# The mask of every other pair of heads added to the bias by GpSimd instead of by a TensorE product

## What is computed

```python
q = (x @ Wq + bq).reshape(B, S, N_HEAD, HEAD_DIM).transpose(0, 2, 1, 3)
k = (x @ Wk + bk).reshape(B, S, N_HEAD, HEAD_DIM).transpose(0, 2, 1, 3)
v = (x @ Wv + bv).reshape(B, S, N_HEAD, HEAD_DIM).transpose(0, 2, 1, 3)
scores = jnp.einsum('bhqd,bhkd->bhqk', q / math.sqrt(HEAD_DIM), k)
scores = scores + attention_bias
scores = jnp.where(src_mask, -jnp.inf, scores.astype(jnp.float32))
probs = jax.nn.softmax(scores, axis=-1).astype(v.dtype)
ctx = jnp.einsum('bhqk,bhkd->bhqd', probs, v)
x = x + (ctx.transpose(0, 2, 1, 3).reshape(B, S, D) @ Wo + bo)
h = _ln(x) * g2 + beta2
return x + (_gelu2(h @ W1 + b1) @ W2 + b2)
```

## Time and profile before

| | us |
|---|---|
| median of 3 runs | 1448.05 |
| lowest and highest | 1447.22 and 1448.72 |
| the profiled execution | 1434.4 |
| its span, which the rows refer to | 1432.6 |

### The profile page before, as it was taken

One profiled execution on the slowest core, in us unless ns is written; L12 is line 12 of the kernel. 1 busy time (PEld: TensorE's weight loads), 2 busy tenths in 40 slices (PEclk: granted clock), 3 DMA queues, 4 the chain that ended last, 5 costly groups with the idle time before them and its releaser, 6 DMA issues. The chain is left out here.

```text
span 1432.6 us, 34478 instructions
## 1 busy us (share of the span) xinstructions
PE 1273.8 (89%) x9923; PEld 1165.2 (81%) x9923; DVE 990.3 (69%) x2766; ACT 899.0 (63%) x2318; POOL 664.5 (46%) x580
## 2 busy tenths in 40 slices
PE   5874899999999999935799999899998999999996
PEld 4774899999999999934587888778887877788875
DVE  5776788879887888646565667666765667666652
ACT  3442777778777877711666676666665666667661
POOL 2775577777777777742132332322332232331211
PEclk9999999999999999967999999999999999999998
DMA  5885121221112112146766555655665556654620
GB/s 194 270 269 188 43 65 48 57 63 55 55 49 64 55 47 65 42 153 196 226 200 200 178 180 192 215 185 171 185 205 185 171 180 204 203 189 149 192 68 15
DMA packets 184851, 203.18 MB, mean 142 GB/s; under 512 B 18192, under 2 KB 172752, under 8 KB 184720
## 3 DMA queue, kind: packets, MB, share of 16 engines
q1 hardware_dynamic: 170832, 163.14, 36.8%
q10 hardware_dynamic: 7712, 21.89, 4.8%
q0 software_dynamic: 6176, 16.79, 3.3%
HBM read 155.89 MB, written 41.68 MB: 138 GB/s over the span
## 5 line engine op out<-in xcount | busy, mean ns | idle before, releaser
L1224 ACT ACTIVATE bias<-bias,neg_max 128x256 f32<-128x256 f32 x512 | 255.4, 501 | 207.6 <-DVE neg_max L1536 207.0
L343 POOL TENSOR_TENSOR w_lo<-w,w_hi 128x512 fp32r<-128x512 f32 x156 | 241.2, 1567 | 0.0
L1536 DVE CUSTOM_DVE_ANT_0 bias<-ps_s,bias 128x256 f32<-128x256 f32 x512 | 194.3, 417 | 28.6 <-PE ps_s L1312 11.1
L745 DVE TENSOR_TENSOR w_lo<-w,w_hi 128x512 fp32r<-128x512 f32 x156 | 149.9, 1000 | 70.2 <-ACT w_hi L423 68.6
L544 PE MATMUL ps_y<-w_hi,hidT_hi 128*128 128x256 f32 x624 | 180.1, 289 | 1.9 <-DVE token_rows L759 1.9
L531 PE MATMUL ps_h<-htokT_hi,w_hi 128*128 128x256 f32 x624 | 178.4, 286 | 3.2 <-DVE htokT_lo L750 3.2
L1310 PE MATMUL ps_s<-mask_f,minus_ident 128*128 128x256 f32 x512 | 154.9, 324 | 28.5 <-DVE neg_max L1536 16.3
L1176 POOL TENSOR_TENSOR act_lo<-up_f,act_hi 128x512 fp32r<-128x512 f32 x64 | 82.6, 1290 | 208.4 <-ACT act_hi L1268 208.4
L531 PE MATMUL ps_h<-htokT_lo,w_hi 128*128 128x256 f32 x624 | 178.2, 286 | 0.0
L531 PE MATMUL ps_h<-htokT_hi,w_lo 128*128 128x256 f32 x624 | 178.0, 285 | 0.0
L544 PE MATMUL ps_y<-w_hi,hidT_lo 128*128 128x256 f32 x624 | 177.1, 284 | 0.0
(11 more groups left out here) (271 smaller groups left out, 3546.9 us busy)
## 6 DMA issues: line engine op xcount, KB each, us to landing
bias<-bias_dram SPq DMA_DIRECT2D x128, 512.0 KB, 4.2
w<-w_dram ACTq DMA_DIRECT2D x32, 512.0 KB, 5.3
xin<-dispatch SPq DMA_DIRECT2D x39, 256.0 KB, 2.7
expert_out<-token_rows SPq DMA_DIRECT2D x39, 256.0 KB, 2.2
q_stack<-q_hi_rows SPq DMA_DIRECT2D x64, 128.0 KB, 3.0
k_stack<-k_hi_rows SPq DMA_DIRECT2D x64, 128.0 KB, 2.9
q_stack<-q_lo_rows SPq DMA_DIRECT2D x64, 128.0 KB, 2.9
k_stack<-k_lo_rows SPq DMA_DIRECT2D x64, 128.0 KB, 2.8
```

The source lines that it names most:

```text
L343: pool.tensor_tensor(w2_part["lo"][:, k, :], w2_piece(e, k), w2_part["hi"][:, k, :].bitcast(F32), ALU.subtract).then_inc(sem("w2_split"), 1)
L745: dve.tensor_tensor(w1_part["lo"][:, k, :], w1_piece(e, k), w1_part["hi"][:, k, :].bitcast(F32), ALU.subtract).then_inc(sem("w1_split"), 1)
L1224: act.activation(head_rows(h, j), head_rows(h, j), ACT.Exp, scale=-1.0, bias=neg_max[par][:, h, j:j + 1], accum_out=total[par][:, h, j:j + ...
L1536: dve.tensor_tensor_reduce(head_rows(h, j), ps_s[h % 2][:, j * T:(j + 1) * T], head_rows(h, j), -1.0, LARGEST, ALU.add, ALU.min, neg_max[p ...
```

## The change

Four of the eight pairs of heads, those with an even number (0, 2, 4, 6), no longer get their mask from TensorE. For them line 1310 is not issued, and the product of queries and keys opens the bank itself. Instead GpSimd adds the mask to the pair's bias in the ring, both heads in one instruction over 128 partitions x 1024 elements (mask_bias). It waits for the landing of the pair and for the mask of the entry, and VectorE's minimum of the pair's first head waits for bias_masked instead of for the landing. So that one table serves both ways, mask_f now holds 0 or -2 to the 127, and the matrix of line 1310 is the plain identity (ident_r). The other four pairs are as before.

```diff
+BY_POOL = (0, 2, 4, 6)
...
-    minus_ident = sb("minus_ident", [P, P], F32R)
+    ident_r = sb("ident_r", [P, P], F32R)
...
-            pool.tensor_scalar(mask_f[par][:], mask[:].bitcast(U8), 1.0, None, ALU.mult).then_inc(sem("mask_taken"), 1)
+            pool.tensor_scalar(mask_f[par][:], mask[:].bitcast(U8), MASKED, None, ALU.mult).then_inc(sem("mask_taken"), 1)
+
+        def mask_bias(n, c, par):
+
+            wait_alone(pool, sem(f"bias_in{c % RING}"), 16 * (2 * n + c // RING + 1))
+            wait_alone(pool, sem("mask_taken"), n + 1)
+            rows = bias[:, c % RING, :, :].rearrange("p h (j k) -> p h j k", j=J)
+            pool.tensor_tensor(rows, rows, spread(mask_f[par][:].bitcast(F32), [P, CHUNK, J, T], 1), ALU.add).then_inc(sem("bias_masked"), 1)
...
         def step(n, par):
+            if exists(n):
+                mask_bias(n, 2, par)
             if exists(n + 2):
                 gather(n + 2)
             if exists(n - 1):
                 rsqrt(rstd2, mv2, "var2_ready", "rstd2_ready", n - 1)
                 prepare_sum(n - 1)
+            if exists(n):
+                mask_bias(n, 4, par)
             if exists(n + 1):
                 take_mask(n + 1, 1 - par)
-            if exists(n - 1):
-                for pair in range(4):
+            for pair in range(4):
+                if exists(n - 1):
                     lower_gelu(n - 1, pair)
+                if exists(n) and pair == 1:
+                    mask_bias(n, 6, par)
+            if exists(n + 1):
+                mask_bias(n + 1, 0, 1 - par)
             if exists(n + 2):
                 rsqrt(rstd, mv, "var_ready", "rstd_ready", n + 2)
...
             for j in range(J):
-                pe.matmul(ps_s[h % 2][:, j * T:(j + 1) * T], minus_ident[:], mask_f[par][:, j, :],
-                          start=True, stop=False)
+                here = h // CHUNK not in BY_POOL
+                if here:
+                    pe.matmul(ps_s[h % 2][:, j * T:(j + 1) * T], ident_r[:], mask_f[par][:, j, :],
+                              start=True, stop=False)
                 last = pe.matmul(ps_s[h % 2][:, j * T:(j + 1) * T], q_stack[par][:, h, j * P:(j + 1) * P].bitcast(F32R),
-                                 k_stack[par][:, h // 2, :].bitcast(F32R), start=False, stop=True)
+                                 k_stack[par][:, h // 2, :].bitcast(F32R), start=not here, stop=True)
...
                 c = h // CHUNK
-                wait_alone(dve, sem(f"bias_in{c % RING}"), 16 * (2 * n + c // RING + 1))
+                if c in BY_POOL:
+                    wait_alone(dve, sem("bias_masked"), len(BY_POOL) * n + BY_POOL.index(c) + 1)
+                else:
+                    wait_alone(dve, sem(f"bias_in{c % RING}"), 16 * (2 * n + c // RING + 1))
...
-            dve.tensor_scalar(minus_ident[:], ident, MASKED, None, ALU.mult)
+            dve.tensor_copy(ident_r[:], ident)
```

## The result

The changed kernel takes 1501.44 us (median of 4 executions, 1500.83 to 1501.87). Beside it the kernel before took 1447.63 us (1445.57 to 1448.72). The ratio is 1.038, with a 95% interval of 1.036 to 1.041: slower by 3.8%, 54 us. Forecast were 1541 us, in a range of 1475 to 1600. The profiled execution has a span of 1500.1 us, against 1432.6 before.

The account below looks back on a forecast made before the run. TensorE was taken to bound slots 7 to 15, VectorE and ScalarE slots 1 to 7. h_rows 30, end of step 53 and clock 10 made +93 on 1434.4, 1527; with 13.65 on top, 1541 us, range 1475 to 1600.

Parts of the forecast that it names:

- the main case: Adds stop VectorE at h_rows and, at the step's end, line 1508 and xn: 1541 us; chance 0.66.
- rival 2: Only h_rows stopped for long: 30 us, 4 for head 12, 0 to 20 for clock; near 1487; chance 0.12.
- the prediction's own list: Signs of being wrong: VectorE's two instructions run before GpSimd's waiting one, adds take 1.3 us, or x3b distance below 46.
- Rival 3: No VectorE instruction of weight stopped, TensorE's gain counts: 15 us less, 1433 us, at best 1417; chance 0.08.
- rival 1: Adds hinder VectorE only as take_mask did, 0.3 us a time: 6 us more, 1454 us; chance 0.07.
- rival 4: Adds on GpSimd cost 3.5 us each: 59 us more, near 1600 us; chance 0.07.
- TensorE's gain, 0.96 us an entry: Slots 7 to 15: 8 of 16 removed matmuls on the path, 0.12 us each, 15 us over 16 entries.
- One add, 2.45 us: GpSimd's time for one 128x1024 mask add, estimated from 128x512 rows; upper end 3.5 us.
- h_rows, +2.0 us an entry: Second norm, behind x3b: pair 4's add delays VectorE's second h_rows, +2.0 us in 15 entries, 30 us.
- The end of the step, +4.1 us an entry: Feed-forward start to query product: adds delay head 12's minimum, line 1508 and xn; 13 entries, 53 us.
- The clock, +10: More TensorE idle time brings a clock dip in ten entries more, 1.0 us each: +10 us, between 0 and 42.
- The lead-in: Ahead of the first entry: no cost counted; gains at the ends, under 1 us, left out.

Follow-up runs that it names:

- e4_no_adds: Kernel after with GpSimd's adds replaced by copies of 2 elements, mask of even pairs left out: 1455.24 us, ratio 1.0119.
- e9_idle_products: Kernel without the adds (2-element copies instead), with the 256 products of the even pairs issued again but idle: 1450.08 us, ratio 1.0065.
- e6_one_input: Kernel after with each add replaced by a one-input multiplication by 1.0 in place: 1487.24 us, ratio 1.0342.
- e14_only_pair4: Kernel after with only the add of pair 4 real, the other three being copies of 2 elements: 1473.03 us, ratio 1.0239.
- the first four runs: Kernel after with pair 4's add moved, pair 2's moved, three moved, or all adds left out: 1474.55, 1491.79, 1481.71, 1455.24 us.

## Why the prediction was right, and where it was not

**The sign** was right, and so was the mechanism at h_rows: TensorE's products were cheap, and adds that stop VectorE cost several times as much. But what the traces show is not the main case, to which 0.66 was given; it is rival 2, to which 0.12 was given: h_rows is stopped for long, head 12 is late, and line 1508 gets ahead of the add in all entries, xn in all but two. Line 1508's two instructions running through before GpSimd's waiting one was a sign of being wrong by the prediction's own list. The 1501.44 us lie at the upper end of what rival 2 gives (1448 and 30, 4 and 20), and 40 us below the 1541 of the sum. Rival 3 (nothing is stopped), rival 1 (stopped as by take_mask) and rival 4 (3.5 us an add) fell. That the range from 1475 to 1600 holds the result is owed to its reaching down over rival 2. On sizes, the profiled spans differ by 67.5 us, of which the steps had 93:

- **TensorE's gain, 0.96 us an entry:** right where the clock stays up, and hardly collected. Between the two kernels with idle products ahead of the feed-forward, the entries at the full clock take 22.2 us without the 8 products and 23.15 with them, a difference of 0.95; the means over all entries are 0.3 us apart (22.86 and 23.16), since the kernel without the adds still has dips. Without idle products it was a loss of 0.5% (e4_no_adds against e9_idle_products): longer dips took back in that stretch what the products gave (24.64 and 24.57). Beside the adds it was 0.4 us an entry (50.4 against 50.1), 4 us between the medians and 9 by the ratios (1.0443 against 1.0382).
- **One add, 2.45 us:** 2.42. The Trainium skill's price (GPSIMD Engine Reference, section 3.1) gave an estimate of 2.25, under the shortest of the 64, 2.33.
- **h_rows, +2.0 us an entry:** 1.73, and moved away it was wholly gone. The second instruction took 2.43 us. Here the rule of the Trainium skill (SBUF — State Buffer, "Who interferes with whom"), that the second comer waits for the whole instruction, and the trace agree: h_rows ended 0.16 us behind the add. With one input they don't agree, as take_mask's row had said and e6_one_input shows, where h_rows ended 1.6 us before GpSimd's instruction; there the measurement decides.
- **The end of the step, +4.1 us an entry:** the step that failed. It was 2.05, and about half of that is the clock (next point). The minimum of head 12 did come late, by 1.28 us of waiting. But line 1508 started 0.27 us ahead of the fourth act_lo, where before it was 0.12 behind the earlier trace rows; so it was a turn ahead of the add too, took 1.92 us, and the add became the longer one, 2.58. xn was stopped in two entries of 16, both ahead of the first x3b (mean 537 ns, against 411), since the add still waited for its pair's landing, 1.66 us behind the rsqrt in the entry shown; the prediction had the pair landed 0.8 us ahead of the rsqrt's end. The add stopped the inverse instead, which is worth 0.4 us. I had argued the two meetings of VectorE and GpSimd as certain, each with 2.45 us. They were each a race decided by tenths of a microsecond, and my own working had moved both sides of the first, VectorE by 0.65 us and act_lo by 0.76, which left line 1508 0.01 us behind.
- **The clock, +10:** under-rated. I expected dips in ten entries more at 1.0 us; from 830 to 1280 us there is one in every entry. The kernel before itself shows the price of one: from feed-forward to query its three entries with a dip take 24.4 to 24.7 us, the others 23.0 to 23.2, so 1.3 to 1.6 us, and ten more are some 15 us. Counted by matmuls, some twelve an entry start 0.09 us later than at the full clock, 1.1 us. Both are estimates from the starts.
- **The lead-in:** left out, with the words that the ends are under 1 us. The first x3b came at 740.41 us instead of 728.94. DVE's timeline of after, at the first add, with the constants of the feed-forward:

```profile
650.34 0.76 DVE L1595 TENSOR_TENSOR v_pad<-ps_q,bv 128x256 f32<-128x256 f32 x2 [0.49 <-PE ps_q L1417]
651.02 2.56 DVE L1656 TENSOR_SCALAR probT<-const,vec 128x128 f32<-128x128 f32 x2
660.38 1.29 DVE L1665 TENSOR_TENSOR probT<-ps_p,probT 128x512 f32<-128x512 f32 x2 [6.80 <-PE ps_p L1462]
```

  The first add (650.90 to 653.24) stopped the making of probT for 2 us (2.56 us for 0.59 before), and behind that wait TensorE's eight products of 512 columns ran from 653.63 to 660.34, 6.7 us at a clock of 0.61 to 0.63, instead of from 651.34 to 655.04, 3.7 at 1.00. That is 5 us, of the 11 in the two steps ahead of the first entry. With pair 4's as the only real add (e14_only_pair4) the first x3b comes at 729.39, so the 11 us belong to the adds of the other pairs.
- **Profile and median:** I put the 13.65 us by which the median stood above the profiled execution on top. For the kernel after the two agree (1501.87 in the profiled execution, median 1501.44), so the forecast was 14 us high by this alone. The next section says what those 13.65 us most likely were.
- **What a measurement can tell:** the chances took 0.2%. The kernel before by itself spread from 1430.33 to 1445.78 us, 1.1%. The result is clear of that; the forecasts of rivals 1 and 3 would not have been.

On the profiled spans, the 93 were 30 for h_rows, 53 for the end of the step and 10 for the clock. Measured, entry by entry, are 26.3 for h_rows (15 entries), 27.5 from feed-forward to query with the clock in it (13 entries), 3.3 in the two entries that have no query product, 11.5 for the lead-in, 0.3 behind the last x3b and 1.3 less in the third stretch: the 67.5. The forecast stood 40 us above the result: 14 by the median, and 26 by steps that were too high by more than the lead-in, which was left out, made up for. That the lead-in stood against them is luck.

## What to carry to other kernels

Work moved from the busiest engine to an idle one can be paid by a third, here VectorE, whose instructions take turns with GpSimd's: cost it by the instructions that it can meet, and when a meeting is decided by tenths of a microsecond, give both outcomes, since every shift upstream deals them anew. Before counting a removed matmul as gain, look whether TensorE's clock falls nearby; here 96 idle products ahead of a wait were worth more than the 256 removed. Sum over the lead-in as well as the steady entries.

## What the hardware did that I had not expected

**A fifth of a microsecond, and the clock.** A copy of 2 elements on GpSimd made h_rows' second instruction 0.16 us longer. With it came a dip of the clock in nine of ten entries instead of three of eleven, at 1.3 to 1.5 us each; the mean granted clock of whole executions went from 0.963 to 0.976 down to 0.958 to 0.966, and the time up by 0.65%. That the first brought the second is argued, not shown. Taking 256 products away on top made the dips longer (0.941 to 0.945) and brought no gain but a loss of 0.5%; adding 96 idle ones at the right place gave 2.1% back.

**The spread of the kernel before is its clock.** Beside the first four runs its 11 executions took 1430.33 to 1445.78 us, the fastest at a mean granted clock of 0.978 and the slowest at 0.964, the others nearly in order between. With the idle products the six executions took 1429.55 to 1431.8 us, at 0.976 to 0.979: they hold the kernel at the time of its best executions. So the 13.65 us between the profiled execution and the median were most likely dips of the clock, and no constant to be carried over; this is read from the order of times and clocks in other executions, not from a trace of a slow one, and of those first three only the profiled one has its clock on record.

**Not always in turns.** Beside a GpSimd instruction of one input, h_rows' second instruction took 1.12 us for 0.69 and ended 1.6 us before the other, which took 2.81 us, where the 64 of its kind took 2.76 to 2.94. Whether the two ran at once, or VectorE's waited for a part of the time, the rows can't tell. Behind the two-input adds in the same place it ended 0.16 us after them.
